# Writing a table of 12,672 rows with 99 indirect scatters in place of 33 direct DMAs

## The reference

```
h = relu(layernorm(x))
x = x + segment_sum(h[dst] * (shifted_softplus(edge_attr @ W1 + b1) @ W2 + b2), src)
h = relu(layernorm(x))
x = x + conv2(relu(conv1(h)))          # relational convolutions, 8 edge types
```

## Time and profile before

| what | value |
|---|---|
| runs | 8896.30 and 8907.12 us, median 8901.71 us |
| profiled execution, span from the first to the last instruction | 8900.7 us |
| profiled execution, time of its own beside the span | not listed |
| mean granted clock of TensorE | 0.674 of full speed |
| `prepare` | 0 to about 262 us |
| filter layer | from about 262 to about 3400 us |
| first table and convolution | about 3400 to 6400 us |
| second table and convolution | about 6400 to 8901 us |

### The profile page before, as it was taken

One profiled execution on the slowest core, in us unless ns is written; L12 is line 12 of the kernel. 1 busy time (PEld: TensorE's weight loads), 2 busy tenths in 40 slices (PEclk: granted clock), 3 DMA queues, 4 the chain that ended last, 5 costly groups with the idle time before them and its releaser, 6 DMA issues. The chain is left out here.

```text
span 8900.7 us, 135914 instructions
## 1 busy us (share of the span) xinstructions
PE 4865.2 (55%) x27214; PEld 3657.4 (41%) x27214; DVE 3631.8 (41%) x12057; ACT 3244.1 (36%) x8454; POOL 5975.5 (67%) x5343
## 2 busy tenths in 40 slices
PE   0677777787777777544444444444933333333332
PEld 0455556565656554333333333333422222222322
DVE  4555555555555556644444444444511111111111
ACT  2655555555555556422222222222422222222222
POOL 3688888888888885566666666665066666666665
PEclk7889888889888988655555555555955555555555
DMA  5555555555555557411111111111511111111112
GB/s 166 123 84 84 85 84 83 84 84 83 83 85 84 84 81 242 142 43 42 42 43 43 43 42 43 42 43 41 235 45 45 45 45 45 45 45 45 45 45 67
DMA packets 574932, 663.22 MB, mean 75 GB/s; under 512 B 108065, under 2 KB 433801, under 8 KB 574577
## 3 DMA queue, kind: packets, MB, share of 16 engines
q0 software_dynamic: 355024, 350.07, 24.0%
q1 hardware_dynamic: 217366, 311.65, 10.9%
q10 hardware_dynamic: 2496, 1.02, 0.1%
HBM read 406.44 MB, written 255.87 MB: 74 GB/s over the span
## 5 line engine op out<-in xcount | busy, mean ns | idle before, releaser
L1162 POOL DMA_INDIRECT got<-table_dram,cidx x3328 | 3170.5, 953 | 2077.3 <-ACT cidx L1210 1092.2
L884 POOL DMA_INDIRECT acc_dram<-total,idx x1664 | 2600.9, 1563 | 538.9 <-issue 341.0
L1195 PE MATMUL bank<-got,share 128*128 128x128 f32 x6656 | 1672.6, 434 | 1635.9 <-ACT share L1220 893.8
L1195 PEld LDWEIGHTS bank<-got,share 128*128 128x128 f32 x6656 | 1453.4, 323 | 1913.3 <-ACT share L1220 1072.4
L1210 ACT ACTIVATE cidx<-srccol 128x4 int32 (+1 forms) x832 | 168.5, 203 | 3261.8 <-remote 2623.3
L1220 ACT ACTIVATE share<-cto_node,etcol 128x128 f32<-128x128 bf16 x3328 | 1082.0, 396 | 538.7 <-DVE cto_node L1274 399.7
L213 DVE SCALAR_TENSOR_TENSOR xs<-bank,mask_hi,xs 128x128 f32 x416 | 146.0, 351 | 2020.3 <-remote 1544.4
L1179 PE MATMUL bank<-cwin,cto_edge 128*128 128x24 bf16 x1664 | 128.0, 192 | 1394.2 <-DVE cwin L1242 1130.9
L850 DVE TENSOR_TENSOR msg<-bank,factor 128x512 f32<-128x512 f32 x416 | 287.8, 692 | 1246.6 <-issue 986.2
L775 ACT ACTIVATE total<-bank 128x258 f32<-128x258 f32 x832 | 275.5, 384 | 1215.2 <-DMA acc_dram<-total,idx 1215.2
L1179 PEld LDWEIGHTS bank<-cwin,cto_edge 128*128 128x128 bf16 x1664 | 88.4, 120 | 1516.2 <-DVE cwin L1242 1207.9
(11 more groups left out here) (164 smaller groups left out, 7729.0 us busy)
## 6 DMA issues: line engine op xcount, KB each, us to landing
edges<-in_edge_attr SPq DMA_DIRECT2D x415, 256.0 KB
table_dram<-made SPq DMA_DIRECT2D x196, 512.0 KB, 2.7
got<-table_dram,cidx POOLq DMA_INDIRECT x3328
win<-split_dram SPq DMA_DIRECT2D x416, 96.0 KB
acc_dram<-total,idx POOLq DMA_INDIRECT x1664
acc_dram<-zeros SPq DMA_DIRECT2D x132, 192.0 KB, 2.1
sums<-acc_dram SPq DMA_DIRECT2D x196, 64.0 KB, 3.3
sums<-acc_dram POOLq DMA_DIRECT2D x196, 64.0 KB, 3.2
```

The lines of the kernel that those rows point to most:

```text
L884: pool.indirect_dma_start(g.acc_dram[j][:, :], bass.IndirectOffsetOnAxis(ap=idx[k][:, j:j + 1], axis=0), total[k][:, j, 0:F], None, comput ...
L1162: pool.indirect_dma_start(got[k][:, j, :], None, g.table_dram[:, :], bass.IndirectOffsetOnAxis(ap=idx[k][:, j:j + 1], axis=0)).then_inc(s_ ...
L1195: ins = nc.tensor.matmul(window[k], share[k][:, j, :], got[ka][:, j, :], start=j == 0, stop=j == TG - 1)
```

## The change

The store of a chunk becomes three indirect scatters of 128 rows each, one for each block, 99 in all. The row numbers come from a new tile `row_i` with one column for each block, made by an iota: partition p of column i holds 128 i + p, so the rows written are the same as before. The semaphore of a split buffer now rises by 48 for a chunk, and the waits for it are scaled. GpSimd's loop over the chunks is written out. The iota raises `s_iota` to 7, and GpSimd waits for that itself.

```
+        row_i = sb("row_i", [P, NBX], I32)
...
+            nc.gpsimd.iota(row_i[:, :], [[P, NBX]], base=0, channel_multiplier=1).then_inc(s_iota, 1)
...
+            pool.wait_ge(s_iota, 7)
...
-                need(act, s_split_out[k], used * 16)
+                need(act, s_split_out[k], used * (16 * CB))
...
-            to = g.split_dram.rearrange("(c b p) f -> c p b f", b=CB, p=P)
-
-            def store(c, k, used):
+            for c in range(NCH):
+                k = c % NSP
                 pool.wait_ge(s_part3, c + 1)
-                chunk = to[c] if isinstance(c, int) else to[bass.ds(c, 1)].rearrange("a p b f -> p (a b) f")
-                pool.dma_start(chunk, split[k][:, :, :, :].rearrange("p b k f -> p b (k f)")).then_inc(s_split_out[k], 16)
-
-            for_chunks(pool, store)
+                for b in range(CB):
+                    i = c * CB + b
+                    pool.indirect_dma_start(g.split_dram[:, :], bass.IndirectOffsetOnAxis(ap=row_i[:, i:i + 1], axis=0),
+                                            split[k][:, b, :, :].rearrange("p k f -> p (k f)"), None).then_inc(s_split_out[k], 16)
             for k in range(NSP):
-                pool.wait_ge(s_split_out[k], 16 * len(range(k, NCH, NSP)))
+                pool.wait_ge(s_split_out[k], 16 * CB * len(range(k, NCH, NSP)))
```

## The result

The changed kernel took 8984.5 us (8980.4 and 8988.7) against 8901.7: a ratio of 1.0093, 95% interval 1.0077 to 1.0110, so +83 us, 0.9%. Two repeats gave 1.0094 (1.0077 to 1.0111) and 1.0100 (1.0083 to 1.0117). The profiled execution took 8988.7 us with a span of 8986.9.

What follows compares the result with a forecast made beforehand. ScalarE paces the store stage at 2.12 us a chunk; 99 scatters at 1.245 us make GpSimd its bound. Next stage at 315.7 in place of 261.66, +54.0 on 8900.7, plus 1.0 from span to median: 8956 us, range 8920 to 9022.

Steps and rivals of the forecast that it cites:

- the tail: From the last store's issue to the next stage's first instruction: 6.46 us as before, plus 0.19 for the longer last issue.
- the gather's 1.245 us: Convolutions' gather of 128 rows, start to start; taken as each scatter's price, so the last scatter starts at 309.0 us.
- the dear row: The filter layer's accumulating scatter, 1.85 us start to start; the upper bound, set aside because its addition belongs to it alone.
- Rival 1: In the store stage, scatters cost as much as accumulating ones: +114 us, 9016; chance 0.25 including prices in between.
- rival 2: Store stage: below 0.70 us start to start, scatters hide behind ScalarE, time stays 8902; chance 0.12 with what lies below.
- rival 3: Store stage: VectorE blocks GpSimd's descriptor making, 3.07 us per scatter, 9137; by the skill's figures some 9160; chance 0.04.
- the loop of buffers: Store stage: waiting for four split buffers takes 9.3 us against GpSimd's 11.2; GpSimd stays the bound until landings take 6.5.
- their limit: DMA engines in the store stage: clears and scatters together 73 of 123 us, so they cease to be near full.
- The filter layer changes nothing: The filter layer, paced by GpSimd's own scatters, starts some 50 us later but keeps its length.

Runs made afterwards that it cites:

- no_add: The changed kernel with the filter layer's 1664 accumulating scatters writing in place of adding: 7246.9 us, against 8086.9 for the kernel before on the same chip.
- rows64: The changed kernel with every scatter cut into two of 64 rows, 198 in all, same bytes: 8266.7 us, on the chip where the kernel before takes 8087.
- direct99: The changed kernel with 99 direct DMAs of 128 rows, without row numbers, in place of the scatters: 8896.2 us, ratio 0.9999 to the kernel before.
- buffers6: The changed kernel with six split buffers in place of four: 8978.6 us.
- unroll33: The kernel before with its 33 direct DMAs, GpSimd's loop written out as in the change: 8087.0 us against 8086.9, ratio 1.0000.

## Why the prediction was right, and where it was short

The forecast was 8956 us, +54; measured were 8984.5, +83. The side, the bound of the stage and the price of one scatter were right; three terms of the sum were missing or too small: the pauses, the tail and the filter layer. The result lies outside the band that I thought likeliest (8945 to 8968, 0.57) and in the one that I kept for dearer scatters (0.25), but it came there by these terms; dearer and stretched scatters were 5 us of it. That the range of 8920 to 9022 holds it is owed to its width.

- **The price of a scatter.** I took the gather's 1.245 us from start to start, and kept 0.56 and 1.85 as bounds. It is 1.267 where nothing disturbs, 2.2 us more over 98. `no_add` shows the reason that I gave for leaving the dear row (the addition is what it pays for), and also the one for leaving out the row's length: its scatters of 512-byte rows took 962 ns and those of 768-byte rows 963. `rows64` shows that the number of rows matters little. Rival 1 is ruled out, and so is rival 2 (`direct99` is that case, and it takes a direct DMA to be in it; the pause of 0.30 us stood behind every scatter). By its own terms rival 3's last figure would have been 9169 us, not some 9160.
- **GpSimd as the bound, not the four buffers.** Right: in `no_add`, which has the preparation of the change, a scatter landed 2.4 us after its issue, at most 3.4, against the 6.5 at which the loop of buffers would have taken over; the profile of the change lists no landing times. `buffers6` moved nothing. The DMA engines were further from their limit than I had said, 0.48 and 0.44 busy (the windows above) in place of 0.6 to 0.7: the 99 scatters took 19.9% of the 144 us from 186 to 330, which is 29 us and not 37.
- **The step that was too small: scatters without a gap between them.** I let ScalarE run ahead of GpSimd and counted no pause, as every register instruction of the stage before was short. On this kind of chip it pauses; 14.1, 11.5 and 12.6 us of gaps in three runs. On the second chip this term was zero, and the next stage began 64.5 us later than in `unroll33`, where I had said 54.
- **VectorE beside the scatters (rival 3).** It did not decide, but it isn't zero. In the timeline of the change all 57 scatters without VectorE beside them took 0.96 us; of the 42 that overlap one of its instructions, 20 took 0.99 to 1.34 and the others 0.96 or 0.97. One that was stretched, with its neighbours:

```profile
200.39 0.96 POOL L568 DMA_INDIRECT split_dram<-split,row_i  x1 [0.30 <-issue]
...
201.42 0.56 DVE L553 TENSOR_TENSOR rest<-h,split 128x384 f32<-128x384 f32 x1 [3.45 <-issue]
201.66 1.16 POOL L568 DMA_INDIRECT split_dram<-split,row_i  x1 [0.30 <-issue]
...
201.90 0.55 DVE L548 TENSOR_TENSOR split<-rest,split 128x384 bf16<-128x384 f32 x1
203.12 0.96 POOL L568 DMA_INDIRECT split_dram<-split,row_i  x1 [0.31 <-issue]
```

  The longest was 1.34 us, the mean 0.993 against a median of 0.963, so 3 us in all. The Trainium skill, SBUF — State Buffer, section SBUF: two separate sides, has the port pair that the two share as an exclusive lock: whoever comes second is blocked for the whole of the other's instruction, also where VectorE has two inputs in SBUF, as here, if the GpSimd operation reads SBUF. The timeline agrees in part, as only scatters beside VectorE were longer, but 22 of 42 were not. The 3100 ns beside a VectorE copy, which the section behind it gives, was not seen; 1338 ns was the most, beside subtractions.
- **The tail.** I moved it over unchanged, 6.46 us and 0.19. It became 10.9, since the drain grew from 2.77 to 8.16 us with the number of DMAs, while the last landing came a microsecond sooner. +4.3 us that no row of before, with 33 DMAs, could show.
- **"The filter layer changes nothing."** Wrong by 6 to 12 us: from first to last scatter it took 3118.6, 3112.4 and 3116.1 us in the three profiles of the change, 3106.2 before. With scatters in the preparation its own scatters had a median of 1552 or 1553 ns in every run (nine profiles, `no_add` left out), with 33 direct DMAs 1545 and 1546, with 99 direct 1541, and with none from GpSimd 1547; times 1664, 7 ns are 12 us. That it goes with the scatters ahead of it, and not with their number or the code, is shown; how is open.

The prediction also says that two per cent is about what a measurement of this kernel can tell from no change. The 13 runs of the kernel before on each chip lie within 0.14% of their median, and +0.9% is clear of that.

The sum put right for the profiled execution: 54.0, + 2.2 for the price, + 3.0 for stretched scatters, + 14.1 for gaps, + 4.3 for the tail, - 0.4 for the start, = 77.2 at the barrier; + 12.4 for the filter layer, - 3.4 for the rest, = 86.2 on the span.

## What to carry to other kernels

An indirect DMA without an addition cost its issuing engine 0.89 us with 64 rows and 0.96 with 128, and a pause of 0.3, against 0.54 for a direct one of the same rows; so contiguous rows belong in one direct DMA, and if they must be scattered, then with all 128 rows in each. Before splitting a DMA in three, set three issues against the pace of the engine that feeds them (2.12 us here): 3 x 0.54 fits and is free, 3 x 1.27 doesn't and is paid in full. A tail at a barrier holds a drain that changes with what was issued (2.8 us after 33 DMAs, 8.2 after 99), so it isn't to be carried over as a constant.

## What the runs showed that I had not expected

**One kernel, two times by the chip.** The kernel before takes 8898 us on one kind of chip and 8087 on the second, 811 us or 9% less, each within 0.14%. VectorE's register and load instructions in the convolutions show the difference (the same line of the helper that adds a window, first the kernel before on the chip of its profile, then `unroll33` on the second):

```profile
L208 DVEq SEQ_ASSERT  x1248: 2/23/1404, 278.3 to 8871.0; - x179
```

```profile
L208 DVEq SEQ_ASSERT  x1248: 23/23/33, 276.2 to 8050.1; - x179
```

On the first kind of chip instructions of a queue that should take 23 to 74 ns sometimes take 0.7 or 1.4 us, in clusters, in the preparation with scatters and in the first convolution with its gathers; in the preparation with 33 or 99 direct DMAs none did, and on the second chip none did in either. In the second convolution of the kernel before none on this line of VectorE's was slow. Both convolutions lose time in the same place: GpSimd waits for ScalarE's index tile before it can gather. The rows for the second convolution, first the kernel before on the chip of its profile, then `unroll33`:

```profile
POOL got L1162 <- ACT cidx L1210: 332.5, 85, 5.6
```

```profile
POOL got L1162 <- ACT cidx L1210: 1.2, 4, 0.3
```

Over the whole span that wait is 1092.2 us and 271.6 in `unroll33`, 821 us less, as much as the time. So here too GpSimd was starved by ScalarE. ScalarE and VectorE stood there at waits that the profile doesn't name ("remote", 1453.3 and 1524.7 us in the second convolution), where on the second chip they waited for TensorE (1456.8 and 1659.0 us); this is another label and not a loss of that size. Nearly all of the 811 us lies in the two convolutions: the gathers run from 3640.6 to 8865.9 us on the one and from 3637.2 to 8049.6 on the other. What makes the chips differ isn't shown by these runs, nor whether the slow instructions and the late ScalarE of the second convolution have one cause.

**The price of an addition at the destination.** 1664 scatters without it took 962 ns in place of 1552, and the layer 900 us less, which is more than all else that was tried here moved.
